# A window-attention layer in batches of 16 units: the first norm and its turning moved into the MLP phase, through device memory

## What is computed

```python
h = _ln(win, ln1_g, ln1_b)
q = jnp.einsum('ntc,chd->nthd', h, wq) + bq
k = jnp.einsum('ntc,chd->nthd', h, wk) + bk
v = jnp.einsum('ntc,chd->nthd', h, wv) + bv
scores = jnp.einsum('nqhd,nkhd->nhqk', q, k) * (1.0 / np.sqrt(KD))
attn = jax.nn.softmax(scores, axis=-1)
o = jnp.einsum('nhqk,nkhd->nqhd', attn, v)
win = win + jnp.einsum('nqhd,hdc->nqc', o, wo) + bo
h2 = _ln(win, ln2_g, ln2_b)
win = win + jax.nn.gelu(h2 @ w1 + b1, approximate=False) @ w2 + b2
```

## Time and profile before

| what | value |
|---|---|
| median of 3 runs | 5121.04 us (5121.0 to 5125.81) |
| profiled execution, span | 5118.4 us |
| PE busy | 4931.8 us, 96% |
| DVE busy | 4072.6 us, 80% |
| ACT busy | 3873.0 us, 76% |
| POOL busy | 3623.5 us, 71% |
| granted TensorE clock | full in all 40 slices |
| one batch, table load to table load | 316.5 us: attention about 180.6, MLP about 135.9 |

### The profile page before, as it was taken

One profiled execution on the slowest core, in us unless ns is written; L12 is line 12 of the kernel. 1 busy time (PEld: TensorE's weight loads), 2 busy tenths in 40 slices (PEclk: granted clock), 3 DMA queues, 4 the chain that ended last, 5 costly groups with the idle time before them and its releaser, 6 DMA issues.

```text
span 5118.4 us, 275139 instructions
## 1 busy us (share of the span) xinstructions
PE 4931.8 (96%) x103124; PEld 4154.1 (81%) x103124; DVE 4072.6 (80%) x9254; ACT 3873.0 (76%) x8206; POOL 3623.5 (71%) x3589
## 2 busy tenths in 40 slices
PE   7999999999999999999999999999999999999999
PEld 6888888888888888888888888887888888888887
DVE  8969778697786977869788796887968879698786
ACT  7859688595886958769587695976949769496794
POOL 6868667686676866767767677676776767777676
PEclk9999999999999999999999999999999999999999
DMA  3141331313213132131322314223042230422304
GB/s 109 34 119 54 94 94 42 116 48 102 86 48 116 42 111 77 56 113 37 117 74 62 112 33 123 68 68 109 26 123 68 74 108 24 124 65 77 108 26 122
DMA packets 222028, 410.68 MB, mean 80 GB/s; under 512 B 29225, under 2 KB 131850, under 8 KB 221898
## 3 DMA queue, kind: packets, MB, share of 16 engines
q1 hardware_dynamic: 220336, 409.06, 27.0%
q10 hardware_dynamic: 1562, 0.50, 0.0%
HBM read 208.11 MB, written 201.33 MB: 80 GB/s over the span
## 4 chain that ended last, share of the span: by engine, by line
PE 55%; DVE 16%; DMA 9%; issue 8%; SPq 7%; ACT 2%; DVEq 2%; POOL 1%; ACTq 0%; POOLq 0%
PE psum L576 12%; PE psum L702 6%; PE psum L591 6%; PE psum L622 6%; PE psum L651 5%; PE psum L608 5%; PE psum L688 5%; PE psum L637 5%; DMA oT<-turned_rows 5%; DMA turned_rows<-normed 4%; SPq L269 4%; PE psum L544 4%; DVE normed L1002 3%; SPq L275 2%; DVE normed L1009 2%
## 5 line engine op out<-in xcount | busy, mean ns | idle before, releaser
L340 POOL TENSOR_TENSOR probs<-probs,prob_inv 128x512 f32<-128x512 f32 x771 | 783.1, 1043 | 839.6 <-DVE prob_inv L982 836.2
L988 DVE TENSOR_TENSOR stream<-stream,psum 128x384 f32 (+1 forms) x1024 | 547.1, 549 | 298.5 <-PE psum L702 225.0
L750 ACT ACTIVATE normed<-stream,shift,rstd 128x96 f32 (+1 forms) x2072 | 770.5, 461 | 17.8 <-issue 16.1
L902 DVE BATCH_NORM_STATS2 stats<-stream 128x6 f32 (+2 forms) x4224 | 721.3, 243 | 58.0 <-DVE stream L988 29.4
L379 POOL TENSOR_TENSOR rstd<-variance,minus_half 128x8 f32<-128x8 f32 (+2 forms) x201 | 745.0, 3707 | 15.7
L347 POOL TENSOR_TENSOR hT<-hT_upper,hT_lower 96x1024 f32<-96x1024 f32 x258 | 614.2, 2380 | 11.8 <-DVE hT_lower L951 6.8
L702 PEld LDWEIGHTS psum<-w_w,gelu_odd 128*64 128x64 f32 x12288 | 512.4, 137 | 59.4 <-issue 59.4
L974 DVE TENSOR_REDUCE prob_sum<-probs 128x8 f32<-128x512 f32 x771 | 492.5, 678 | 84.2 <-ACT probs L784 84.1
L966 DVE TENSOR_TENSOR probs<-psum,row_max 128x512 f32<-128x512 f32 x771 | 533.2, 692 | 26.6
L830 ACT ACTIVATE gelu_odd<-psum 128x512 f32<-128x512 f32 x768 | 418.7, 593 | 174.8 <-PE psum L688 156.5
L702 PE MATMUL psum<-w_w,gelu_odd 128*64 128x96 f32 x12288 | 536.4, 247 | 12.2 <-ACT gelu_odd L830 12.2
(11 more groups left out here) (94 smaller groups left out, 11327.9 us busy)
## 6 DMA issues: line engine op xcount, KB each, us to landing
turned_rows<-normed SPq DMA_DIRECT2D x624, 128.0 KB
stream<-in_x SPq DMA_DIRECT2D x272, 192.0 KB
out<-stream SPq DMA_DIRECT2D x256, 192.0 KB
stream<-in_x SPq DMA_DIRECT2D x272, 180.0 KB
out<-stream SPq DMA_DIRECT2D x256, 180.0 KB
probsT<-turned_rows SPq DMA_DIRECT2D x112, 384.0 KB, 3.2
oT<-turned_rows SPq DMA_DIRECT2D x112, 384.0 KB, 3.2
turned_rows<-gelu_odd SPq DMA_DIRECT2D x144, 128.0 KB
```

Of the source, the lines that this page charges most:

```text
L340: nc.gpsimd.tensor_tensor(block_h, block_h, inv, ALU.mult).then_inc(probs_ready, 1)
L750: last = nc.scalar.activation(normed1[:, t, :], stream[:, slot, t * C:(t + 1) * C], ACT.Identity, bias=shift1[:, index, t:t + 1], scale=rs ...
L902: last = nc.vector.bn_stats(stats[:, index, c, :], stream[:, slot, c * C:(c + 1) * C])
L988: nc.vector.tensor_tensor(part, part, psum[:, banks[g], 0:GROUP], ALU.add).then_inc(added, 1)
```

## The change

The first norm of a unit is no longer made in the attention step three steps ahead of its use. For units 3 to 15 of the next batch `normalise1` runs on ACT in the MLP steps of the batch before, DVE turns the rows in 32x32 blocks (`turn_h1`, one instruction), SP sends them to device memory in one transfer of 384 KB (`send_h1`), and in the attention phase SP fetches each unit back (`fetch_h1`, three transfers of 128 KB) into one of two buffers `h_raw`, two steps after the unit that used that buffer. Units 0 to 2 are normed and turned in attention steps 8 to 13 of the batch before. Batch 0 has all of it in its own attention phase, with five steps ahead of it.

- PE loses `transpose1` (8 instructions a unit). `project_v` reads `h_raw` and, since its tokens now stand in another order, does 32 products of 32 tokens instead of 16 of 64.
- ACT's `hT_upper` copies read `h_raw` instead of PSUM; the second copy of k now stands ahead of them and so ahead of v's copies.
- The subtraction `hT_lower` moves from DVE (reading PSUM) to POOL (reading SBUF), behind the scaling of the probabilities; `unite_hT` goes.
- DVE gets `turn_h1` in MLP steps 3 to 15, between `turn_h2` and the statistics. It waits until the transfer of the unit before has landed (`h1_left`), since there is one buffer `turned1_late`.
- SP loads one unit in each attention step instead of 16 in a burst. In MLP steps `send_h1` stands between the store and the fetch.
- `probsT` now lies in `gelu_odd`, and `turned_late` in the second half of `probs`.

The core of the diff:

```diff
+            def send_h1(u, source):
+                wait_apart(sp, h1_turned, u + 1)
+                slot = u % SLOTS if isinstance(u, int) else u & (SLOTS - 1)
+                sp.dma_start(turned1_dram[slot].rearrange("b p x -> p b x"),
+                             source.rearrange("p (b x) -> p b x", b=CBLOCKS)).then_inc(h1_left, 16)
+            def fetch_h1(u, parity):
+                if not (isinstance(u, int) and u < 2):
+                    wait_apart(sp, v_done, 2 * (u - 1))
+                wait_apart(sp, h1_left, 16 * (u + 1))
...
+                for cb in range(CBLOCKS):
+                    sp.dma_start(h_raw[parity][BLOCK * cb:BLOCK * (cb + 1), :]...,
+                                 turned1_dram[slot, cb]...).then_inc(h1_back[parity], 16)
...
-            def unite_hT(u):
...
+            def copy_hT_lower(u, parity):      # POOL
+                for g in range(2):
+                    pool.wait_ge(hT_upper_copied, 2 * u + g + 1)
+                    nc.gpsimd.tensor_tensor(lower[:, tokens], h_raw[parity][0:C, tokens], upper[:, tokens],
+                                            ALU.subtract).then_inc(hT_copied, 1)
...
             def project_qk(u, n):
                 if n == 0:
-                    pe.wait_ge(hT_copied, 2 * (u + 1))
+                    pe.wait_ge(hT_copied, 2 * u + 1)
...
                         for side in range(2):
-                            last = nc.tensor.matmul(
-                                psum[WT * side:WT * (side + 1), V_BANKS[g], t * C:(t + 1) * C],
-                                hT[:, tokens], qkv_w[:, 2, :], start=True, stop=True)
+                            for part in range(2):
+                                at = part * SHARES + (2 * (4 * g + t) + side) * BLOCK
+                                keys = WT * side + BLOCK * part
+                                last = nc.tensor.matmul(
+                                    psum[keys:keys + BLOCK, V_BANKS[g], t * C:(t + 1) * C],
+                                    h_raw[parity][:, at:at + BLOCK], qkv_w[:, 2, :], start=True, stop=True)
...
-                for g in range(2):
-                    transpose1(u + 3, g)
...
+            def turn_h1(u, turned):            # DVE
+                if not (isinstance(u, int) and u == 0):
+                    wait_apart(dve, h1_left, 16 * u)
+                dve.wait_ge(ln1_ready, u + 1)
+                nc.vector.transpose(turned..., normed1...).then_inc(h1_turned, 1)
...
                     turn_h2(batch + j + 3, turned_late, False)
+                    if turns:
+                        turn_h1(batch + BATCH + j, turned1_late)
                     statistics1(batch + BATCH + AHEAD + j, AHEAD + j, batch_row + BATCH_ROWS + row, half)
```

More of the change, by code:

```diff
@@ L323, in _ @@
-            with sp.Fori(0, BATCH_ROWS) as r:
-                for half in (0, 1):
-                    load(BATCHES * BATCH_ROWS + r, r, half)
-            store_batch((BATCHES - 1) * BATCH_ROWS)
+                for i in range(BATCH - 4):
+                    n = i % RING
+                    send_turned(batch + i + 4, turned_late, n)
+                    store(batch_row + i // 2, i % 2)
+                    if i >= 2:
+                        send_h1(batch + BATCH + i + 1, turned1_late)
+                    fetch_late(batch + i + 4, n)
@@ new lines, in _ @@
+            mlp_traffic(0)
+            with sp.Fori(1, BATCHES) as b:
+                batch_row = b * BATCH_ROWS
+                batch = b * BATCH
+                for s in range(BATCH):
+                    if s in (10, 12, 14):
+                        send_h1(batch + BATCH + (s - 10) // 2, turned1_early)
+                    fetch_h1(batch + s + 3, (s + 3) % 2)
+                    row = batch_row + BATCH_ROWS + s // 2
+                    load(row, row & (WROWS - 1), s % 2)
+                    if s in (6, 9, 11):
+                        n = (6, 9, 11).index(s)
+                        send_turned(batch + n, turned_early, n)
+                    if s in (7, 10):
+                        n = (7, 10).index(s)
+                        fetch_turned(batch + n, raw_early[n], n)
+                mlp_traffic(batch_row)
@@ L509, in mlp @@
                 add_b2(batch)
+                if first:
+                    finish2(call, batch + 6, 6, 2)
+                    call = call + 1
                 for j in range(BATCH):
@@ L816, in attention_step @@
                     copy_qk(front, 2)
-                for g in range(2):
-                    copy_hT_upper(u + 3, g)
+                    copy_qk(front, 3)
+                copy_hT_upper(u + 3, 1 - half)
                 if not absent(front):
@@ L865, in _, with attention @@
+            def attention(batch):
                 nc.scalar.preload_act_table_set("natural_log_exp_and_others")
-                with act.Fori(0, BATCH_ROWS) as r:
+                with act.Fori(0, 4) as r:
                     for half in (0, 1):
-                        attention_step(batch + 2 * r + half, half, (2 * r + half + AHEAD) & (BATCH - 1))
+                        attention_step(batch + 2 * r + half, half)
+                for s in range(8, 14):
+                    attention_step(batch + s, s % 2)
+                    if s % 2 == 0:
+                        n = (s - 8) // 2
+                        normalise1(batch + BATCH + n, n)
+                for s in range(14, BATCH):
+                    attention_step(batch + s, s % 2)
@@ L879, in _ @@
                 gelus(batch + BATCH - 1, 1, 1)
+            mlp(0)
+            with batches(mybir.EngineType.Activation, 1) as b:
+                attention(b * BATCH)
+                mlp(b * BATCH)
         @block.vector
```

362 lines of the change are left out of this document (183 added, 179 removed).

## The result

The changed kernel takes **5499.9 us** (median of 4 runs, 5492.8 to 5509.0), the kernel before 5121.5 (median of 4, 5121.0 to 5125.8): a ratio of 1.0739, 95% interval 1.0723 to 1.0754. That is 378 us more; the forecast was +269, with the range up to 5580. Its profiled execution spans 5495.1 us.

A forecast was written before the change was run, and what follows sets the result against it. PE and ACT were taken as both full in attention, PE as setting the MLP pace. MLP +242 (DVE's chain), attention +15 and start +15, together +272 on 5118.4 plus 2.6, gave 5390 us, range 5100 to 5580.

The forecast's parts named there:

- A light attention step: Attention: ACT's list up to v's first copy keeps the step at 10.6 us, hiding 0.85 us of v's extra cost.
- I add 0.2 on the mean: Attention: steps with more DVE work delay the exponentials by up to 0.5 us; mean step 10.85 against 11.02.
- the +1 for units 0 to 2: Attention: three steps of a batch carry a `normalise1`; ACT's idle time hides most of it, +1 us a batch.
- The entry: Start of a batch's attention: the first `fetch_h1` stands where loads started, scores at 1644.1 instead of 1641.5, +2.6 us a batch.
- v's own cost: Attention, PE: 64 records of half the weight columns instead of 32, +0.15 us, bounds 0 and +1.37.
- rival C: Attention, PE: v costs twice, +1.37 us less 0.85 hidden, +130 us on the forecast, 5520 us; chance 0.08.
- just in time: Attention: POOL's two subtractions, after its scaling of the probabilities, counted as not late; any lateness left to the range.
- DVE's chain: MLP: `turn_h1` waits for the landing of the unit before, holding DVE's step; 9.75 us a step, +242 us in all.
- ACT's chain: MLP: `normalise1` before the next gelus makes them 1.9 us late over three steps, 9.1 us a step, +117 us.
- The landing of `send_h1`: MLP: the transfer behind six stores lands in 3.9 us, high bound 6.4, thus 10.9 us after the turn.
- The start: Start with batch 0: unit 0 makes a trip through memory and batch 0 keeps `normalise1` in its attention, +15 us.
- Rival B: Attention: v's first copy is ready by 9.75 us, steps shrink by 1.07 us, -257 us, total 5020 us; chance 0.17.

The follow-up runs named there:

- v ahead: In ACT's attention step the two copies of v stand ahead of the two `hT_upper` copies, against the changed kernel: 5309.1 us.
- the six kernels between 9.31 and 9.48: The kernel with v's copies ahead of `hT_upper` and five built on it, with edits to DVE's, POOL's, ACT's or SP's order: 5285.7 to 5324.3 us.
- The best kernel here: SP's entry fetch ahead of its wait for stores, on a kernel with v's copies first, POOL's b2 last and gelus ahead of `h2T_upper`: 5285.7 us.
- the slowest kernel: In ACT's MLP step `normalise1` stands ahead of `h2T_upper`, in the wait for the fetch, against the changed kernel: 5955.6 us.

## Why the prediction was right, and where not

The direction, the range and the mechanism of a light attention step held; the forecast was 110 us low, 77 of them in attention (+92 against +15), 22 in the MLP phases and 12 at the start, and its reason for the MLP phase was not the one that sets the time.

- **A light attention step** was forecast at 10.6 us with PE waiting for v's copy; it takes 10.65. "v ahead" shows that ACT's order is the cause: -191 us.
- **Heavy steps.** The term "I add 0.2 on the mean" is too small. The 14 steps behind the entry take 1932.69 - 1777.07 = 155.6 us, 11.11 each, against the 10.85 forecast (the same 14 took 11.05 before): 0.46 above the lightest, 10.65. Where PE waits 1.56 us for v's copy instead of 0.76, that it comes by the exponentials, which move everything behind them in ACT's list, is argued, not shown. These steps take 3.7 us a batch more than 14 of 10.85, and the +1 for units 0 to 2 covers only one of them.
- **The entry** was forecast at +2.6 us. The scores start 1777.07 - 1761.09 = 16.0 us apart, 5.4 more than before, and this is most of what attention lost. The forecast let the fetch be issued where the loads were, 1637.32 - 1630.86 = 6.5 us behind the start of the scores; it is issued 1770.26 - 1761.09 = 9.2 behind it. What the term left out is SP's jump to its next batch, 2.4 us, which the kernel before does not have at this place. The wait for the stores, 1.1 us, was in it.
- **v's own cost** was +0.09 us (forecast +0.15, bound 1.37): rival C is out.
- **POOL "just in time"** was half a microsecond or more off, which showed only when v no longer hid it.
- **The MLP phases** cost +264 against +242, but that they came so near is luck. The forecast laid its loss on 12 of 16 steps; 16.5 us over 12 is 1.37 each, 9.86 a step if all of it lies there, above both chains (9.1 for ACT, 9.75 for DVE's landing). And the step that put DVE's chain as the later one fails: with its wait gone the kernel was 40 us slower, and a shorter `normalise1` won 122, where ACT's chain was sized at 117. ACT's wait for fetches, "mostly gone" by the forecast, is 576 us of 895. The landing of `send_h1`, forecast at 3.9 us, was not the error, though the page has less in the median:

```profile
turned_rows<-probs SPq DMA_DIRECT2D x208, 384.0 KB, 2.8
```

  Read one by one, the 96 sends behind six stores land in 2.8 us (median) and the 96 behind two stores in 4.2, such as that of 1984.74, for which DVE waits until 1989.50; those that DVE waited for took 3.9 in the mean. Left out were the wait for POOL's shift and the clock, whose fall the forecast had named as a sign of being wrong. What makes up the other 0.46 us is open: part is the clock (4.9 of 16.5 us a phase), the rest lies in waits that hand over to each other as one is taken away, as the six kernels between 9.31 and 9.48 suggest.
- **The start** cost 27 us, forecast 15; it was not looked into.
- **Rival B** (PE gets what it lost) needed v's copy 0.85 us sooner. Even with v put ahead, attention falls only to 177.0 us against 180.6 before, and 16 MLP steps cost more than that (13.4).

The parts that were measured apart are 191 (ACT's order in attention, 31 of them in the MLP phases), 122 (the norm's time in the MLP phase) and 39 (the fetch ahead of the wait for the stores). They were measured on different kernels and overlap at the entry, where "v ahead" frees v's copy from the fetch too, so they do not add up to a share of the 378. The best kernel here, 5285.7 us, is still 3.2% above the one before. SP's jump at the entry was in every version and was not tested.

## What to carry over

Taking work from the engine that is busiest gains nothing if another engine's in-order list delivers, a few instructions later, what that engine wants next; follow that list up to the copy that is wanted, and put that copy first. An instruction moved into a phase with idle time brings its own waits into the list: ask what stands behind it there, and who finishes its inputs. A transfer that an engine waits for is only as early as its issuer: look at what SP does just before it, its jumps too. In a ring of several engines that hand over to each other, exchanging two instructions can cost more than the whole change (456 us here against 378), so look for the wait that each exchange closes into a ring before looking for the one that it opens.

## What the runs showed of the hardware

- **Waits cost PE twice.** In windows of 10 us the granted clock was 0.89 and then 0.94 around and after the wait of 4.05 us, and 0.50 with the one of 6.44 us. The mean clock is 0.998 before, 0.976 after, and 0.941 in the slowest kernel (5955.6 us, span 5950.2), where PE is busy 5020 us with the same instructions that take 4829 in "v ahead".
- **DVE and POOL hold each other up** on operations that read SBUF: a subtraction that takes 0.94 us at the least took 3.57 beside POOL's operations of 1.29 and 1.84, and a small POOL operation 0.96 us where the next of its shape takes 0.23.
- **One transfer of 384 KB** that spreads over all partitions lands in 2.8 us (median), and in 4.2 when only two stores stand between it and the three sends ahead of it. The send of as much in three transfers by 32 rows, in the attention phase before, is waited for another 4.6 us after 1.8 us of issuing.
- **SP's jump to the head of its loop over the batches** is followed by 2.45 to 2.78 us without an instruction of SP (14 jumps of the changed kernel), while whatever it should issue next waits.
